# Recurrence and feed-forward layer norms by per-token statistics instructions in a fused early-fusion model kernel

## What is computed

```python
def _layernorm(x, axis=-1, eps=1e-05):
    m = jnp.mean(x, axis=axis, keepdims=True)
    v = jnp.var(x, axis=axis, keepdims=True)
    return (x - m) / jnp.sqrt(v + eps)
...
    h = x @ Win.T + bin_
    for l in range(L):
        h = _ssm_layer(h, A[l], Bm[l], Cm[l], Dm[l])   # ends with: y = gelu(y) + h; return _ln(y)
    h = _ln(h)
    return h @ Wout.T + bout
...
    h = h + _L0_attn_ref(_layernorm(h), ...)   # the recurrence
    h = h + _L0_ffn_ref(_layernorm(h), ...)    # the feed-forward
    h = h + _L1_attn_ref(_layernorm(h), ...)
    h = h + _L1_ffn_ref(_layernorm(h), ...)
```

## Time and profile before

| | us |
|---|---|
| median of three runs (562.21 to 565.05) | 562.22 |
| the profiled execution, device time | 569.07 |
| its span, first to last instruction | 567.2 |
| TensorE / VectorE / ScalarE / GpSimd busy | 419.8 / 271.9 / 159.6 / 93.7 |
| mean granted TensorE clock, share of full speed | 0.807 |

### The profile page before, as it was taken

The page is one execution under the profiler, slowest core; times in us unless marked ns, Lnnn a source line. Parts: engine busy times, 40 slices in busy tenths (PEclk is TensorE's granted clock), DMA queues, the critical chain, the costliest instruction groups (busy, mean ns, idle before and its releaser), DMA issues.

```text
span 567.2 us, 10216 instructions
## 1 busy us (share of the span) xinstructions
PE 419.8 (74%) x4178; PEld 279.9 (49%) x4178; DVE 271.9 (48%) x669; ACT 159.6 (28%) x333; POOL 93.7 (17%) x106
## 2 busy tenths in 40 slices
PE   9754968796687774568899999999783379988200
PEld 5733737374254442346357777777632253477200
DVE  1355484642425445565546666666436630077122
ACT  2223436262122222302234544444300000144000
POOL 3202020000201112111400000000020077000375
PEclk9567878778769998555789999999986658999655
DMA  8360000000530000000560000000010000132111
GB/s 330 162 245 2 3 2 5 2 18 3 138 77 1 2 1 0 1 0 28 181 293 1 3 5 5 5 5 5 5 31 1 1 25 25 43 102 92 38 41 34
DMA packets 19735, 27.83 MB, mean 49 GB/s; under 512 B 12680, under 2 KB 17416, under 8 KB 19048
## 3 DMA queue, kind: packets, MB, share of 16 engines
q1 hardware_dynamic: 16144, 23.86, 12.2%
q0 software_dynamic: 1536, 1.58, 1.1%
q10 hardware_dynamic: 2016, 1.84, 1.0%
HBM read 21.50 MB, written 6.03 MB: 49 GB/s over the span
## 4 chain that ended last, share of the span: by engine, by line
PE 59%; DVE 21%; ACT 6%; POOL 5%; issue 4%; DMA 3%; DVEq 1%; POOLq 0%; SPq 0%; ACTq 0%
PE bank L1163 49%; PE bank L1166 10%; POOL windows L504 4%; DVE q_sum L784 3%; DVE windows L1134 1%; POOL rstd L451 1%; DVE xT L882 1%; ACT xT L614 1%; DMA hL<-tokens_in 1%; DVEq L1131 1%; ACT xT L726 1%; DVE xT L899 1%; DVE sc_sb L807 1%; DVE sc_sb L811 1%; DVE head_buf L791 1%
## 5 line engine op out<-in xcount | busy, mean ns | idle before, releaser
L1163 PE MATMUL bank<-windows 65*64 65x64 f32 (+3 forms) x976 | 94.0, 263 | 2.3 <-DVE windows L1134 1.9
L1163 PE MATMUL bank<-zero 128*64 128x512 f32 x130 | 71.8, 707 | 2.5 <-DVE hL L1119 1.1
L1163 PEld LDWEIGHTS bank<-windows 65*64 65x64 f32 (+3 forms) x976 | 65.2, 150 | 4.6 <-ACT windows L722 3.1
L451 POOL TENSOR_TENSOR rstd<-ln_v,mhalf 128x6 f32<-128x6 f32 x16 | 21.1, 1326 | 173.6 <-DVE ln_v L877 173.6
L1032 DVE TENSOR_REDUCE xT<-bank 96x2 f32<-96x384 f32 (+1 forms) x48 | 26.5, 552 | 45.4 <-PE bank L1163 45.4
L689 ACT ACTIVATE head_buf<-head_buf 96x384 f32<-96x384 f32 x48 | 25.1, 523 | 66.5 <-DVE head_buf L1035 66.5
L1163 PEld LDWEIGHTS bank<-zero 128*64 128x64 f32 x130 | 19.7, 161 | 48.0 <-issue 45.6
L1166 PE MATMUL bank<-w_tok,xT 128*128 128x128 f32 (+2 forms) x104 | 18.9, 319 | 32.0 <-DVE xT L882 20.0
L1166 PEld LDWEIGHTS bank<-w_tok,xT 128*128 128x128 f32 (+2 forms) x104 | 12.9, 152 | 45.9 <-DVE xT L882 27.5
L1163 PE MATMUL bank<-xT 64*64 64x64 f32 (+2 forms) x192 | 31.6, 310 | 1.5 <-issue 0.7
L504 POOL DMA_INDIRECT windows<-y_slots,addr x24 | 22.8, 948 | 56.2 <-SPq L420 49.2
(11 more groups left out here) (212 smaller groups left out, 635.2 us busy)
## 6 DMA issues: line engine op xcount, KB each, us to landing
big<-in_x SPq DMA_DIRECT2D x4, 2048.0 KB, 11.6
big<-in_w_experts SPq DMA_DIRECT2D x1, 6144.0 KB, 18.1
x_slots<-zero SPq DMA_DIRECT2D x1, 1792.0 KB, 10.8
windows<-x_slots SPq DMA_DIRECT2D x14, 128.0 KB, 2.1
y_slots<-windows ACTq DMA_DIRECT2D x14, 128.0 KB, 1.7
w_ssm<-in_w_ssm SPq DMA_DIRECT2D x1, 448.0 KB, 8.6
hL<-tokens_in SPq DMA_DIRECT2D x2, 192.0 KB, 2.3
tokens_in<-hL SPq DMA_DIRECT2D x2, 192.0 KB, 1.8
```

What stands on the lines that cost most here:

```text
L451: pool.tensor_tensor(stat(rstd, k), stat(ln_v, k), mhalf[:, 0:L], ALU.pow).then_inc(s["ln_rstd"], 1)
L1163: return nc.tensor.matmul(out, lhsT, rhs, start=start, stop=stop, **kw)
```

## The change

Each layer norm of n = 0 to 7 gets its mean and variance from one `bn_stats` per token (64 channels in, six numbers out) and one `bn_aggr` per token (six in, mean and variance out), six of each for a half; one small instruction adds epsilon. The centred tile and the squares on ScalarE go. `norm_c` becomes six `tensor_scalar` instructions, one per token, which subtract the mean and multiply by `rstd` in one pass, both read per partition from SBUF. `norm_b` is gone, and the variance is ready at the end of `norm_a`. `add_bout` on GpSimd now waits for the normalised tile instead of the centred one. The layer norm ahead of the experts (L1050 to L1058) is untouched.

```diff
--- before.py
+++ after.py
@@ -170,6 +170,8 @@
         hs = over(1, [128, LT, D])
         uT = over(1, [128, 2, HPAIR * 128])
         ln_s = sb("ln_s", [128, LT])
+        ln_parts = sb("ln_parts", [128, LT, 6])
+        ln_mv = sb("ln_mv", [128, LT, 2])
         ln_m = sb("ln_m", [128, LT])
         ln_q = sb("ln_q", [128, LT])
         ln_v = sb("ln_v", [128, LT])
@@ -452,7 +454,7 @@
 
             def add_bout(k):
 
-                pool.wait_ge(s["ln_centered"], nth(k, 0))
+                pool.wait_ge(hf["u_ready"][k], 1)
                 pool.wait_ge(s["wssm_in"], 16)
                 pool.tensor_tensor(half(hL, k), half(hL, k), ws("bout").unsqueeze(1).broadcast_to([128, L, D]),
                                    ALU.add).then_inc(s["hLb_ready"], 1)
@@ -604,10 +606,6 @@
                     scan_matrices(p + 1)
             tokens_out(PAIRS - 1)
 
-            def squares(k, n):
-                act.wait_ge(s["ln_centered"], nth(k, n))
-                nc.scalar.activation(half(sq, k), half(xc, k), ACT.Square).then_inc(s["ln_squared"], 1)
-
             def u_blocks(k, r):
 
                 act.wait_ge(hf["uT_ps"][k], r + 1)
@@ -635,37 +633,25 @@
             def turned_tokens(k):
                 act.wait_ge(s["xN_ps"], nth(k, 0))
                 copy(tokens_of(k, 0, 4), y_bank[k][0:64, :].rearrange("p (i t) -> p t i", i=4)).then_inc(hf["xN_ready"][k], 1)
-            squares(0, 0)
-            squares(1, 0)
             u_blocks(0, 0)
             u_blocks(0, 1)
             for l in range(SSM_LAYERS):
-                if l:
-                    squares(1, l)
-                else:
+                if not l:
                     u_blocks(1, 0)
...
@@ -866,20 +852,21 @@
             add_queries(PAIRS - 1)
 
 
-            def norm_a(k, n, src):
-                link(red(stat(ln_s, k), src, AX.X, ALU.add))
-                link(ts(stat(ln_m, k), stat(ln_s, k), 1.0 / D, None, ALU.mult))
-                tt(half(xc, k), src, across(ln_m, k), ALU.subtract).then_inc(s["ln_centered"], 1)
-
-            def norm_b(k, n):
-                dve.wait_ge(s["ln_squared"], nth(k, n))
-                link(red(stat(ln_q, k), half(sq, k), AX.X, ALU.add))
-                ts(stat(ln_v, k), stat(ln_q, k), 1.0 / D, EPS, ALU.mult, ALU.add).then_inc(s["ln_var"], 1)
-
-            def norm_c(k, n, dst, then):
+            def norm_a(k, src):
+
+                for i in range(L):
+                    ins = nc.vector.bn_stats(half(ln_parts, k)[:, i, :], src[:, i, :])
+                link(ins)
+                for i in range(L):
+                    ins = nc.vector.bn_aggr(half(ln_mv, k)[:, i, :], half(ln_parts, k)[:, i, :])
+                link(ins)
+                ts(stat(ln_v, k), half(ln_mv, k)[:, :, 1], EPS, None, ALU.add).then_inc(s["ln_var"], 1)
+
+            def norm_c(k, n, src, dst, then):
                 dve.wait_ge(s["ln_rstd"], nth(k, n))
-                dve.wait_ge(s["ln_centered"], nth(k, n))
-                tt(half(dst, k), half(xc, k), across(rstd, k), ALU.mult).then_inc(hf[then][k], 1)
+                for i in range(L):
+                    ins = ts(half(dst, k)[:, i, :], src[:, i, :], half(ln_mv, k)[:, i, 0:1], stat(rstd, k)[:, i:i + 1], ALU.subtract, ALU.mult)
+                ins.then_inc(hf[then][k], 1)
 
             def add_bin(k):
                 dve.wait_ge(s["y_ps"], nth(k, 0))
@@ -905,46 +892,37 @@
                 dve.wait_ge(s["h_ready"], nth(k, 0))
 
             dve.wait_ge(hf["tok_in"][0], 16)
-            norm_a(0, 0, half(hL, 0))
+            norm_a(0, half(hL, 0))
             dve.wait_ge(hf["tok_in"][1], 16)
-            norm_a(1, 0, half(hL, 1))
-            norm_b(0, 0)
-            norm_b(1, 0)
-            norm_c(0, 0, y1, "u_ready")
+            norm_a(1, half(hL, 1))
+            norm_c(0, 0, half(hL, 0), y1, "u_ready")
             add_bin(0)
             for l in range(SSM_LAYERS):
                 states(0, l)
-                if l:
-                    norm_b(1, l)
-                else:
-                    norm_c(1, 0, y1, "u_ready")
+                if not l:
+                    norm_c(1, 0, half(hL, 1), y1, "u_ready")
                 scanned(0, l)
                 if not l:
                     add_bin(1)
                 add_skip(0, l)
                 if l:
-                    norm_c(1, l, hs, "u_ready")
-                norm_a(0, l + 1, half(y1, 0))
+                    norm_c(1, l, half(y1, 1), hs, "u_ready")
+                norm_a(0, half(y1, 0))
                 states(1, l)
-                norm_b(0, l + 1)
                 scanned(1, l)
                 add_skip(1, l)
-                norm_c(0, l + 1, hs, "u_ready")
-                norm_a(1, l + 1, half(y1, 1))
+                norm_c(0, l + 1, half(y1, 0), hs, "u_ready")
+                norm_a(1, half(y1, 1))
             dve.wait_ge(hf["u_ready"][0], 6)
-            norm_a(0, 5, half(hs, 0))
-            norm_b(1, 4)
-            norm_b(0, 5)
-            norm_c(1, 4, hs, "u_ready")
-            norm_c(0, 5, y1, "u_ready")
+            norm_a(0, half(hs, 0))
+            norm_c(1, 4, half(y1, 1), hs, "u_ready")
+            norm_c(0, 5, half(hs, 0), y1, "u_ready")
             dve.wait_ge(hf["u_ready"][1], 6)
-            norm_a(1, 5, half(hs, 1))
+            norm_a(1, half(hs, 1))
             add_wout(0)
-            norm_a(0, 6, half(hL, 0))
-            norm_b(1, 5)
-            norm_b(0, 6)
-            norm_c(1, 5, y1, "u_ready")
-            norm_c(0, 6, x2, "x2_ready")
+            norm_a(0, half(hL, 0))
+            norm_c(1, 5, half(hs, 1), y1, "u_ready")
+            norm_c(0, 6, half(hL, 0), x2, "x2_ready")
 
             def token_weights(k):
                 dve.wait_ge(hf["x2_ready"][k], 1)
@@ -981,21 +959,18 @@
                 copy(tokens_of(k, 4, L), f_bank[k][0:64, 0:256].rearrange("p (i t) -> p t i", i=2)).then_inc(hf["xN_ready"][k], 1)
             token_weights(0)
             add_wout(1)
-            norm_a(1, 6, half(hL, 1))
+            norm_a(1, half(hL, 1))
             ranks(0)
-            norm_b(1, 6)
             chosen(0)
-            norm_a(0, 7, half(hL, 0))
-            norm_c(1, 6, x2, "x2_ready")
+            norm_a(0, half(hL, 0))
+            norm_c(1, 6, half(hL, 1), x2, "x2_ready")
             token_weights(1)
-            norm_b(0, 7)
             ranks(1)
-            norm_c(0, 7, x3, "x3_ready")
+            norm_c(0, 7, half(hL, 0), x3, "x3_ready")
             chosen(1)
-            norm_a(1, 7, half(hL, 1))
+            norm_a(1, half(hL, 1))
             turned_tokens(0)
-            norm_b(1, 7)
-            norm_c(1, 7, x3, "x3_ready")
+            norm_c(1, 7, half(hL, 1), x3, "x3_ready")
             turned_tokens(1)
 
             def value(b):
```

More of the change, by code:

```diff
@@ L649, in _ @@
                 u_blocks(1, l + 1)
-                squares(0, l + 1)
                 states(1, l)
@@ L654, in _ @@
                     u_blocks(0, l + 2)
-            squares(1, 4)
-            squares(0, 5)
             u_blocks(0, 5)
-            squares(1, 5)
-            squares(0, 6)
             u_blocks(1, 5)
             u_blocks(0, 6)
-            squares(1, 6)
             hidden_tokens(0)
             u_blocks(1, 6)
-            squares(0, 7)
             hidden_tokens(1)
             turned_tokens(0)
-            squares(1, 7)
             turned_tokens(1)
```

## The result

The changed kernel takes 577.93 us in the median of four runs (575.24 to 582.58), the kernel before 563.63 in the four runs beside them (562.21 to 569.31). The ratio is 1.0243, with a 95% interval from 1.014 to 1.0346: slower by 14 us. The forecast was 565.0 and a range up to 571, so the time lies outside it. The profiled execution took 582.58 us with a span of 580.8, 13.6 more than the profiled span of before.

The account below looks back on a forecast made before the run. The prediction took a serial loop over half-layers to bound the kernel, with only `norm_c` of the norm on its chain. Six terms summed to +2.8 us on the 562.2 us median, giving 565.0, range 560 to 571.

Parts of the forecast that it names:

- What bounds the kernel: One serial loop over half-layers, about 7.05 us a round; of the layer norm only `norm_c` lies on its chain.
- the four places outside it: Where statistics lie on the chain: tokens' arrival, behind the last layer, behind the output projection, behind `ranks(0)`.
- Term 1, arrival: Where the tokens arrive, to the end of `norm_c(0,0)`: 3.07 us instead of 4.13, so -1.06.
- Term 2, the loop: In the recurrence, `norm_c` stands on the chain seven times, each 0.75 us longer: +5.25 us.
- The first rival: TensorE's clock falls in the loop as its idle time ahead of the transposes grows: 569.3 us, chance 0.22.
- the dense products behind the short piece: Argument against the clock falling in the loop: the idle piece is short and 2.9 us of dense products follow.
- The bound of `FF`: In the loop, `FF` is wanted 2.1 us after `norm_c` ends; the new `norm_a`, 1.74 us, fits.
- Terms 3 to 5: Behind the last layer -0.34 us, behind the output projection -0.97, behind `ranks(0)` -0.81.
- Term 6: Behind `ranks(1)`, `norm_c(0,7)` releases the last transposes: +0.75 us; the rest of half 1 hides beside products on zeros.
- The rule on the emptied pipe: Skill's rule that the next VectorE instruction awaits an empty pipe; six scalings would cost 1.52 us, the sum about 2.5 more.
- The cheap rivals: `norm_c` at 0.84 us for six: 559.4 us, chance 0.15; or six for 0.56 us: 556.0 us, chance 0.03.
- the dear one: New instructions are dear, `norm_c` 1.48 us and `norm_a` 2.85, and `FF` comes late: 572.6 us, chance 0.10.

Follow-up runs that it names:

- e3: The kernel before with two idle scalings ahead of the real one for norms 1 to 4, which widens the gap; ratio 1.0104, 572.1 us.
- e7: The kernel before with `norm_c` alone split into six `tensor_scalar`, one operand read per partition, statistics as before; ratio 1.0328, 582.2 us.
- e1: The changed kernel with two products on zeros instead of one at the end of each half-layer; ratio 1.0111, 571.6 us.
- e2: The changed kernel with GpSimd's two memsets for the attention tiles moved to the start of the recurrence; ratio 1.0142, 573.0 us.
- e6: The changed kernel with two products on zeros per half-layer, memsets moved to the recurrence's start, GpSimd's `bo` addition held until the last scaling; ratio 0.9986, 566.7 us.
- e4: The changed kernel, but with the tile centred in one instruction off the chain and `norm_c` one scaling again; ratio 0.981, 555.9 us.
- e8: e4 with `norm_c(1,6)` and `token_weights(1)` moved ahead of `ranks(0)` in VectorE's list; ratio 0.9708, 548.8 us.

## Why the prediction was wrong, point by point

**What bounds the kernel** was right: `norm_c` alone of the norm is on the loop's chain, and the four places outside it were the right ones.

**Term 1, arrival** (-1.06): -1.2, right. What the term missed lies behind it: TensorE was idle for 0.42 us there instead of 1.77 and got its full clock back earlier (it had 0.50 from 156.8 to 160.1 us only and 1.00 from 160.2, where before had 0.51 up to 166.8), so the first layer took 2.3 us less. This is no luck of one run: from the second half's tokens to the first copy of `cT` it takes 16.8 to 17.4 us in the three kernels with the old statistics (before, e3, e7) and 12.6 to 13.4 in the seven with the new ones. That the shorter idle piece is the cause is argued and not shown.

**Term 2, the loop** (+5.25): +12.2 in the profile. This is the step that failed. Its size was off in the price, 1.43 us for six where the prediction took 1.31, seven times 0.12 = 0.8 us; the term's own mechanism gives 6.1. Its cover failed in the clock, which the forecast held at 1.00 ("still at clock 1.00"): 6.1 us more. The first rival said this, with 0.22, and its working was close in kind: 4.3 us for one or two falls of up to 2.9 against three or four of 1.6. Its 569.3 us was still far from the measured time, since it did not have term 6's block either. What I weighed against it, the dense products behind the short piece, did not hold it up. e1 and e3 show the cause from both sides: filling the gap ends the falls, widening it in the old kernel makes them.

**The bound of `FF`** held: VectorE still waits 0.62 us or more ahead of it in every half-layer behind the first; `norm_a` takes 1.61 us, and the forecast had 1.74.

**Terms 3 to 5** (-0.34, -0.97, -0.81): -0.6, -1.1, -0.9. Right, and a little larger: `norm_a` is 0.13 us shorter, `norm_c` 0.12 longer, and the scaling starts 0.09 us before the instruction ahead of it ends (237.92 against 238.01), where the forecast had a hand-over.

**Term 6** (+0.75): +0.9 for `norm_c(0,7)`, right. The sentence behind it, "What follows of half 1 lies beside the five products on zeros", was wrong: the blocked scaling outlasts them. It costs 2.6 us and then 1.6 in attention products at a fallen clock. No rival named it. The forecast counted the memset neither as a neighbour nor as work, since the earlier trace rows and the chain don't show it; the timeline of before has it beside the old scaling, which it left alone. e2 shows that moving it returns most of this, e6 that holding GpSimd's additions back too returns the rest.

**The rule on the emptied pipe** (the Trainium skill, "VectorE: DVE Perf Modes", section "The DRAIN you can't avoid") does not hold here for unlinked neighbours, as argued: instructions of 0.310 us start 0.224 apart. That section says itself that a next instruction which is not held starts earlier, which the prediction left out; so the Trainium skill and the trace agree. The price of six came out near the rule's 1.52 us for another reason, the second operand.

**The cheap rivals** fall: 1.43 us for six, not 0.84 or 0.56. Of the dear one, `norm_c` was near (1.48), `norm_a` not (2.85).

In sum, by the table: the forecast's own terms measure 3.2 us (-1.2, +6.1, -0.6, -1.1, -0.9, +0.9) where the forecast had 2.8. What it had not counted is the clock in the loop, +6.1, the blocked scaling with the slow attention products behind it, +4.2, the first layer, -2.3, and the untouched stretches, +2.4; together 13.6. e6, without the two side effects, is within the noise of the kernel before (0.9986, 0.9938 to 1.0034).

## What to carry to other kernels

Splitting one instruction on the chain into one per token is paid twice: by the operands (50 to 60 ns each here) and by whoever idles meanwhile; look at the granted clock of the engine that waits, and fill the gap before judging the change. Take the gain of a fused statistic where it is off the chain and leave the instruction on the chain whole: e4 does so and gains 1.9% where the change lost 2.4%. When an instruction changes its form, look at what GpSimd runs beside it: the old form may have been the one that was not blocked.

## What the runs showed of the hardware

- A VectorE `tensor_scalar` with SBUF operands on both sides is held up by a GpSimd memset (a 2.66 us one; six scalings in 5.34 us instead of 1.43) and by a GpSimd addition of two SBUF tiles (3.35 us). In the changed kernel the first three scalings end 0.1 to 0.2 us behind the memset, and the fourth and the fifth 0.05 us behind the two additions. A `tensor_tensor` is not held up by the memset (0.56 us beside it, e4), but by a GpSimd addition it is (1.34 instead of 0.56, e8).
- The power on GpSimd over 128x6 held nothing up: six scalings beside it (at 237.92) took 1.42 us in the changed kernel, and the power its usual 1.32. In e4, beside a VectorE subtraction, it took 1.56 us itself instead of 1.33.
- `bn_stats` on 128x64: one lasts 212 ns, a run of six 0.86 us; `bn_aggr` on six numbers: one 155 ns, six 0.51.
- In the loop TensorE lost its full clock where a gap of 1.64 us, transposes of 0.55 and a gap of 0.57 followed each other, but not each time. With 1.27 in place of 1.64 (e7) it did so in two of six half-layers, with 0.77 (before, e1, e6), never.
